# AdaLN, gated recurrence, MLP and conditioned feed-forward on one core: the MLP output made with features on the partitions, and x1 kept in that form for the first feed-forward layer

## The chip, the cores and the metric

The kernel runs on one core of one Trainium2 chip. The metric is the device time of one execution in microseconds (us). The reported time is the median of three runs.

## The reference, cut to what matters

Two sequences of 2048 tokens with 512 features each pass through three stages. Stage 1 is a modulated linear layer and a gated linear recurrence; its result with the residual added is `hs2`. Stage 2 and 3, where the change lies, are

```python
# stage 2, the MLP: x1 is the result
h   = rms_norm(hs2) * norm2_w
g   = gelu(h @ mlp_gate_w.T + mlp_gate_b)
f   = h @ mlp_fc_w.T + mlp_fc_b                 # both 3*512 wide
x1  = x + hs2 + (g * f) @ out_w.T + out_b       # x is the kernel's input
# stage 3, the conditioned feed-forward; _ln(x, g, b) is a layer norm with gain and bias
h = _ln(_ln(x1, pw_g[pathway], pw_b[pathway]), cp_g[compartment], cp_b[compartment])
t = _ln(x1, tm_g[time], tm_b[time]);  s = _ln(x1, ms_g[scale], ms_b[scale])
m, n, r = (x1 + condition_vector[i] for i in range(3))
w = softmax(aw)
cat = concat(w0*h, w1*t, w2*m, w3*n, w4*r, w5*s)
u   = _ln(silu(cat @ int_W1 + int_b1) @ int_W2 + int_b2, int_g, int_be)
out = x1 + int8_matmul(u, rhs)
```

m, n and r are x1 with a vector added, so their three weights are mixed into one and the first layer has four operands: x1, h, t and s.

Products are made in three passes of split operands (high times high, high times low, low times high), so each product of a 128x128 block with 512 columns is three matmuls.

## The kernel before, in words

Everything is cut in eight blocks of 512 tokens (`NB = 8`, `BT = 512`). A block is four tiles of 128 tokens (`TT`) or four tiles of 128 features (`KT`). All five engines run programs written out by hand, joined by semaphores that count up. The functions `two_ahead` and `blocks` (lines 88 and 106) run the first and the last blocks as straight code and those between in a loop, and pass `prev` (a block before this one exists) and `nxt` (one follows) to each body. Stage 2 is `mlp_half` (line 714 on), stage 3 is `conditioned_ffn` (line 1124 on). Stage 3 begins inside the last MLP block: its `early(j)` parts prepare weights and tables, one part behind each feature tile j.

**An MLP block.** TensorE goes through j = 0 to 11 (`FT`), the feature tiles of the 1536 wide layer. For each j it makes the gate product (12 matmuls, `product`, line 848), the fc product (12 matmuls), and then the output product of the tile before (`project_out(j - 1)`, line 863, 12 matmuls). The output product takes `pr` (the split activations) as the stationary operand and `out_w` as the moving one, so its four banks `A[t]` hold tokens on the partitions. `hs2` lies with features on the partitions; `to_tokens` (lines 867 to 878) turns it by 16 transposes per block, four after j = 4, four after j = 5 (`T_AT`), eight after the loop. VectorE adds them to the tile `xt` (128 tokens by 512 features, four of them), into which SyncE has loaded the block of x (line 813), and at the end of the block adds `A[t]` (line 1098). SyncE stores `xt` to `x1_d` in memory (line 820). ScalarE makes Gelu (line 971) and the high part of the product (line 975); VectorE the product (line 1072) and the low part (line 1075).

**SyncE's order in an MLP block** (`body`, lines 810 to 820): wait for the store of the block before, load x, load the next `hs2`; in the last block then `early()` of stage 3 (line 1347), which loads small tables, x1 of block 0, and, once gate and fc of j = 3 are done, the six weights of the condition networks (lines 1362 and 1365: three loads, together 1024 KB, then three of 1024 KB each); then the store of x1. TensorE's part `early(4)` waits for the first three of these six.

**A feed-forward block.** The first layer is a sum over 16 steps `s`: four of x, four of h, and four each of t and s in turn. Each step needs its operand with features on the partitions, split in a high part (ScalarE, `front_high`, line 1650) and a low part (VectorE, `front_low`, line 2036). TensorE makes each by four transposes (`emit`, line 1432): the kinds are "tx" (of x1), "th", "tt", "ts". The 16 of "tx" for the next block stand between the last of the first layer (`main_last`, line 1485, 48 matmuls) and the second layer (`second`, line 1503, 48 matmuls). The second layer ends in the banks `A[t]`, VectorE takes them out (`take_u`, line 2053, semaphore `u_evac`), and the first step of the next block (`main`, line 1466) waits for `u_evac` of each bank before it overwrites it. VectorE's order at the end of a block (lines 2122 to 2127):

```python
            hidden(b)
            if nxt:
                for s in range(XF):          # XF = 4
                    front_low(b + 1, s)
                h_product(b + 1)
                take_u(b)
```

x1 is loaded again in rows (`x1t`, line 1307) for the layer norm, and in `x_residual` tiles (line 1321) for the last addition. GpSimd gathers the time and scale rows by indirect transfers (line 1871) while this goes on.

## Time and profile before

| what | us |
|---|---|
| median of 3 runs | 1853.86 |
| lowest, highest run | 1853.76, 1854.52 |
| the profiled execution, whole | 1854.19 |
| its span, first to last instruction | 1851.1 |
| TensorE busy in the span | 1817.9 |
| VectorE busy | 997.0 |
| ScalarE busy | 733.5 |
| GpSimd busy | 502.6 |

The whole time is 3.1 us more than the span. A time inside the span is counted from its first instruction. Busy time of TensorE is an upper figure, since its matmuls overlap; the distance between the starts of two groups says what a group costs in a stream. The attention stage runs to about 480 us, the eight MLP blocks to about 1285 us, the feed-forward blocks to the end.

### The profile page before, as it was taken

What the parts mean: (1) busy time and instruction counts of PE and PEld (TensorE: products, weight loads), DVE (VectorE), ACT (ScalarE), POOL (GpSimd) and SP (SyncE); (2) the same over time, 40 slices, a digit from 0 to 9 for tenths busy, and PEclk for the clock granted to TensorE, in tenths of its full rate; (3) what the DMA queues carried; (4) which work ended last, traced back from release to release, by engine and by line L of the source; (5) the groups of instructions that cost most, each with busy time, mean ns of one, the idle gap of its engine ahead of it and who ended that gap; (6) DMA issues with size and microseconds to landing.
All of it is one profiled execution on the core that took longest, in us unless ns stands there. A gap on an engine that the chain in (4) does not pass through costs nothing. (4 is left out here: it accounts for less than half of the span.)

```text
span 1851.1 us, 23492 instructions
## 1 busy us (share of the span) xinstructions
PE 1817.9 (98%) x8410; PEld 1483.9 (80%) x8410; DVE 997.0 (54%) x1644; ACT 733.5 (40%) x1117; POOL 502.6 (27%) x502
## 2 busy tenths in 40 slices
PE   7999999999999999999999999999899999999996
PEld 6888888888888888888888888876788888888884
DVE  6767676757743434224242434337775666666555
ACT  6655555556532222222222212224353543533433
POOL 0121222112100000000000000006677876877742
PEclk9999999999999999999999999999999999999998
DMA  5011111013401010101001010453335334324401
GB/s 196 1 46 46 45 45 34 13 46 125 171 1 69 1 69 1 70 1 42 27 3 67 1 69 0 131 192 119 128 126 162 103 125 147 125 92 160 136 12 46
DMA packets 62199, 138.40 MB, mean 75 GB/s; under 512 B 5490, under 2 KB 5746, under 8 KB 62116
## 3 DMA queue, kind: packets, MB, share of 16 engines
q1 hardware_dynamic: 49812, 94.24, 14.8%
q0 software_dynamic: 11776, 41.95, 7.1%
q8 instruction: 58, 0.95, 0.2%
q10 hardware_dynamic: 528, 1.05, 0.2%
q14 instruction: 25, 0.20, 0.0%
HBM read 112.06 MB, written 25.17 MB: 74 GB/s over the span
## 5 line engine op out<-in xcount | busy, mean ns | idle before, releaser
L291 PE MATMUL bank<-h_parts,gate_w 128*128 128x512 f32 x1536 | 351.5, 390 | 0.2 <-DVE h_parts L588 0.2
L291 PEld LDWEIGHTS bank<-h_parts,gate_w 128*128 128x128 f32 x1536 | 288.1, 188 | 61.9 <-issue 1.0
L1072 DVE SCALAR_TENSOR_TENSOR product_full<-bank,vec_sb,gelu 128x512 f32<-128x512 f32 x96 | 72.0, 750 | 408.6 <-PE bank L848 361.4
L1466 PE MATMUL bank<-operand_parts,int_w 128*128 128x512 f32 x1152 | 283.6, 396 | 3.1 <-DVE operand_parts L2036 3.0
L863 PE MATMUL bank<-mlp_out_w,product_parts 128*128 128x512 f32 x1152 | 280.6, 392 | 0.0
L848 PE MATMUL bank<-h_parts,mlp_gate_w 128*128 128x512 f32 x1152 | 276.9, 389 | 0.9 <-DVE h_parts L1055 0.9
L848 PE MATMUL bank<-h_parts,mlp_fc_w 128*128 128x512 f32 x1152 | 276.8, 389 | 0.0
L848 PEld LDWEIGHTS bank<-h_parts,mlp_gate_w 128*128 128x128 f32 x1152 | 216.1, 188 | 46.5 <-issue 1.7
L863 PEld LDWEIGHTS bank<-mlp_out_w,product_parts 128*128 128x128 f32 x1152 | 214.0, 188 | 49.1 <-issue 4.2
L1466 PEld LDWEIGHTS bank<-operand_parts,int_w 128*128 128x128 f32 x1152 | 214.1, 189 | 47.7 <-issue 3.2
L848 PEld LDWEIGHTS bank<-h_parts,mlp_fc_w 128*128 128x128 f32 x1152 | 216.2, 188 | 44.9
L1853 POOL TENSOR_TENSOR fence<-minus_half 128x1 f32<-128x1 f32 x32 | 9.7, 304 | 711.0 <-DVE id_row L2145 707.7
L971 ACT ACTIVATE gelu<-bank,vec_sb 128x512 f32<-128x512 f32 x96 | 66.2, 689 | 281.1 <-PE bank L848 278.5
L975 ACT ACTIVATE product_parts<-product_full 128x512 fp32r<-128x512 f32 x96 | 60.7, 632 | 287.1 <-DVE product_full L1072 284.4
L2036 DVE TENSOR_TENSOR operand_parts<-bank,operand_parts 128x512 fp32r<-128x512 f32 x128 | 85.4, 682 | 73.2 <-ACT operand_parts L1650 73.2
L528 POOL TENSOR_TENSOR decay_sq<-decay 128x512 f32<-128x512 f32 x32 | 37.8, 1180 | 301.6 <-DVE decay L601 301.6
L1075 DVE TENSOR_TENSOR product_parts<-product_full,product_parts 128x512 fp32r<-128x512 f32 x96 | 66.5, 693 | 68.6 <-ACT product_parts L975 68.6
L1485 PE MATMUL bank<-operand_parts,int_w 128*128 128x512 f32 x384 | 90.5, 394 | 0.1
L1503 PE MATMUL bank<-int_w,hidden_parts 128*128 128x512 f32 x384 | 89.0, 391 | 0.0
L1485 PEld LDWEIGHTS bank<-operand_parts,int_w 128*128 128x128 f32 x384 | 72.0, 188 | 16.2 <-issue 0.5
L1650 ACT ACTIVATE operand_parts<-bank 128x512 fp32r<-128x512 f32 x128 | 71.6, 590 | 32.3 <-PE bank L1432 32.2
L1503 PEld LDWEIGHTS bank<-int_w,hidden_parts 128*128 128x128 f32 x384 | 71.6, 188 | 14.5
(272 smaller groups left out, 2307.0 us busy)
## 6 DMA issues: line engine op xcount, KB each, us to landing
xin<-xT SPq DMA_DIRECT2D x8, 1024.0 KB, 7.0
hs_d<-u SPq DMA_DIRECT2D x8, 1024.0 KB, 5.0
x_tiles<-x SPq DMA_DIRECT2D x8, 1024.0 KB, 5.9
x_d<-x_tiles SPq DMA_DIRECT2D x8, 1024.0 KB, 4.5
x_tiles<-x_d SPq DMA_DIRECT2D x8, 1024.0 KB, 8.0
out<-u_tiles SPq DMA_DIRECT2D x32, 256.0 KB, 5.0
raw_w<-int_W SPq DMA_DIRECT2D x7, 1024.0 KB, 7.9
x_residual<-x_d SPq DMA_DIRECT2D x28, 256.0 KB
```

Source lines behind the costliest of these rows:

```text
L291: i = pe.matmul(bank[:], gw[:, w, s, k, m * P:(m + 1) * P], hr[:, q, t, k, :], start=k == 0 and n == 0, stop=k == KT - 1 and n == 2)
L848: i = pe.matmul(bank[:], (gw, fw)[w][j // KT][:, s, k, (j % KT) * P:(j % KT + 1) * P], hr[:, t, k, :], start=k == 0 and n == 0, stop=k == ...
L863: i = pe.matmul(A[t][:], pr[:, j % 2, s, t * P:(t + 1) * P], ow[j // KT][:, w, j % KT, :], start=j == 0 and n == 0, stop=j == FT - 1 and n ...
L971: act.activation(gg[:], G[j % 2][:], ACT.Gelu, bias=v("mlp_gate_b", j)).then_inc(g_evac, 1)
L975: act.activation(pr[:, j % 2, 0, :], pf[:], ACT.Copy).then_inc(p_high, 1)
L1072: dve.scalar_tensor_tensor(out=pf[:], in0=FB[j % 2][:], scalar=v("mlp_fc_b", j), in1=gg[:], op0=ALU.add, op1=ALU.mult).then_inc(p_full, 1)
L1075: dve.tensor_tensor(pr[:, j % 2, 1, :], pf[:], pr[:, j % 2, 0, :].bitcast(F32), ALU.subtract).then_inc(p_low, 1)
L1466: i = pe.matmul(A[m][:], w1[OPER[o]][:, a, k, m * P:(m + 1) * P], op[:, s % 4, c, :], start=s == 0 and n == 0, stop=False)
L1485: i = pe.matmul(A[m][:], w1[OPER[o]][:, a, k, m * P:(m + 1) * P], op[:, s % 4, c, :], start=False, stop=s == NS - 1 and n == 2)
L1503: i = pe.matmul(A[t][:], zr[:, a, k, t * P:(t + 1) * P], w2[:, c, k, :], start=k == 0 and n == 0, stop=k == KT - 1 and n == 2)
L1650: act.activation(op[:, s % 4, 0, :], bank(kind, k)[:], ACT.Copy).then_inc(S["op_high"], 1)
L2036: dve.tensor_tensor(op[:, s % 4, 1, :], bank(FRONT[o], k)[:], op[:, s % 4, 0, :].bitcast(F32), ALU.subtract).then_inc(S["op_low"], 1)
```

## The change

The output product of the MLP has its operands exchanged: `out_w` is the stationary operand and `pr` the moving one, so the banks `A[c]` hold features on the partitions. The last tile's product signals after each bank. x is loaded transposed (`xT`), `hs2` is added to it without a transpose, with the bias in the same instruction (two at j = 6, two at j = 8). x1 is stored with features on the partitions (`x1T_d`), and in the next MLP block its rows are made by 16 transposes, after j = 1, 2, 3, 4, copied out by ScalarE and stored to `x1_d`. For the last MLP block this is done in the first feed-forward block. SyncE's order in the block becomes: load `hs2`, (last block: small loads of stage 3), wait for the store and for the block's transposes, load x, wait for the copies, store the rows, (last block: the weights of stage 3), wait and store x1. The squares, the mean and the normalisation for the next block come at j = 6 and 9 instead of 5 and 7.

In the feed-forward part the "tx" transposes are gone. The four x operands are read from memory: columns 0 and 1 of the next block early in a block, columns 2 and 3 at its end, by transfers of 256 KB that ScalarE issues into the two halves of `xs` once the low parts of columns 0 and 1 are made. VectorE makes the first two low parts, two tiles of the h product, the second two low parts, two tiles of the h product. Some semaphores are merged, with no change of order.

```diff
@@ MLP, numbers @@
-    SQ = 5
-    MS = 8
-    T_AT = {4: 0, 5: 1}
+    SQ = 6
+    MS = 10
+    T_AT = {1: 0, 2: 1, 3: 2, 4: 3}
+    R2_AT = {6: (0, 1), 8: (2, 3)}
+    OB = FT + KT - 1
@@ MLP, sync_program, body @@
+            if prev and nxt:
+                sp.wait_ge(r2, KT * b)
+                load(b + 1, 1 - q)
+            if not nxt:
+                last_small()
             if prev:
                 sp.wait_ge(x_stored, 16 * b)
-            sp.dma_start(xt[:], x_nat[:, bass.ds(TT * b, TT), :]).then_inc(x_loaded, 16)
-            if prev and nxt:
                 sp.wait_ge(t_ps, TT * b)
-                load(b + 1, 1 - q)
+            sp.dma_start(xt[:], xT[:, :, bass.ts(b, BT)]).then_inc(x_loaded, 16)
+            if prev:
+                sp.wait_ge(t_evac, TT * b)
+                sp.dma_start(x1_d[:, bass.ds(TT * (b - 1), TT), :], rows_of[:]).then_inc(t_stored, 16)
             if not nxt:
                 last_early()
-            sp.wait_ge(r1, TT * (b + 1))
-            sp.dma_start(x1_d[:, bass.ds(TT * b, TT), :], xt[:]).then_inc(x_stored, 16)
+            sp.wait_ge(r1, KT * (b + 1))
+            sp.dma_start(x1T_d[:, :, bass.ts(b, BT)], xt[:]).then_inc(x_stored, 16)
@@ MLP, tensor_program @@
-            for t in range(TT):
+            for c in range(KT):
                 for n, (s, w) in enumerate(PASSES):
-                    i = pe.matmul(A[t][:], pr[:, j % 2, s, t * P:(t + 1) * P], ow[j // KT][:, w, j % KT, :],
+                    i = pe.matmul(A[c][:], ow[j // KT][:, s, j % KT, c * P:(c + 1) * P], pr[:, j % 2, w, :],
                                   start=j == 0 and n == 0, stop=j == FT - 1 and n == 2)
-            i.then_inc(o_ps, 1)
...
+                if j == FT - 1 or c == KT - 1:
+                    i.then_inc(o_ps, 1)
+
+        def to_tokens(b, j):
+            t = T_AT[j]
+            pe.wait_ge(r1, KT * b)
+            pe.wait_ge(g_evac, FT * b + j + 1)
             for k in range(KT):
-                i = pe.transpose(T[t][:, k * P:(k + 1) * P], z[q][:, k, t * P:(t + 1) * P], ident[:])
+                i = pe.transpose(G[j % 2][:, k * P:(k + 1) * P], xt[:, k, t * P:(t + 1) * P], ident[:])
             i.then_inc(t_ps, 1)
...
-                if j in T_AT:
-                    to_tokens(b, q, T_AT[j])
+                if prev and j in T_AT:
+                    to_tokens(b, j)
...
-            for t in range(2, TT):
-                if not nxt:
-                    ready(FT)
-                to_tokens(b, q, t)
-            if not nxt:
-                tokens()
@@ MLP, scalar_program @@
+                act.wait_ge(t_stored, 16 * (b - 1))
...
+        def evacuate_rows(b, j):
+            t = T_AT[j]
+            act.wait_ge(t_ps, TT * (b - 1) + t + 1)
+            act.wait_ge(h_low, KT * (b + 1))
+            act.activation(rows_of[:, t, :], G[j % 2][:], ACT.Copy).then_inc(t_evac, 1)
@@ MLP, vector_program @@
-            for k in range(KT):
-                dve.tensor_scalar(z[q][:, k, :], z[q][:, k, :], v("out_b", k), None, ALU.add).then_inc(zb_done, 1)
...
+        def add_hs2(b, q, ks):
+            dve.wait_ge(x_loaded, 16 * (b + 1))
+            for k in ks:
+                dve.scalar_tensor_tensor(out=xt[:, k, :], in0=z[q][:, k, :], scalar=v("out_b", k), in1=xt[:, k, :],
+                                         op0=ALU.add, op1=ALU.add).then_inc(r2, 1)
@@ feed-forward, sync_program @@
-                    sp.wait_ge(S["tx_ps"], KT * (b + 1))
...
-        def early():
+        def early_small():
...
-            sp.wait_ge(mlp["tokens"], TT * (NB - 1))
+            sp.wait_ge(mlp["hs2"], KT * (NB - 1))
+            sp.wait_ge(mlp["tok_stored"], 16 * (NB - 2))
             load(0)
+
+        def early():
             sp.wait_ge(mlp["gate"], LASTJ + KT)
             sp.wait_ge(mlp["fc"], LASTJ + KT)
...
+            for k in range(2, KT):
+                sp.dma_start(xs_first[:, k - 2], x1T_d[:, k, bass.ts(0, BT)]).then_inc(first_loaded, 16)
+            sp.wait_ge(tb_ps, 1)
+            for k in range(2):
+                sp.dma_start(xs[:, k], x1T_d[:, k, bass.ts(0, BT)]).then_inc(xs_loaded[k], 16)
+            sp.wait_ge(S["xh_done"], TT)
+            load(1)
@@ feed-forward, tensor_program @@
+        def last_tokens(ts):
+            pe.wait_ge(mlp["x1"], KT * NB)
+            for t in ts:
+                for k in range(KT):
+                    i = pe.transpose(ring[2 + t % 2][:, k * P:(k + 1) * P], xt[:, k, t * P:(t + 1) * P], ident[:])
+                i.then_inc(mlp["tokens"], 1)
...
-            if nxt:
-                for n in range(NI, len(items)):
-                    item(b, q, n, prev)
@@ feed-forward, scalar_program @@
+        def load_x(b, k):
+            if k < 2:
+                act.wait_ge(S["op_low"], NS * (b - 1) + k + 3)
+            else:
+                act.wait_ge(S["op_low"], NS * b + k - 1)
+            act.dma_start(xs[:, k % 2], x1T_d[:, k, bass.ts(b, BT)]).then_inc(xs_loaded[k % 2], 16)
...
             if nxt:
-                for s in range(XF):
-                    front_high(b + 1, s)
+                x_high(b + 1, 0)
+                x_high(b + 1, 1)
+                load_x(b + 1, 2)
+                load_x(b + 1, 3)
             if not prev:
                 h_centre(b + 1)
-                rhs_round(range(KT))
+                rhs_round(range(2))
+            if nxt:
+                x_high(b + 1, 2)
+                x_high(b + 1, 3)
@@ feed-forward, vector_program @@
-                for s in range(XF):
+                for s in range(0, XF, 2):
                     front_low(b + 1, s)
-                h_product(b + 1)
+                    front_low(b + 1, s + 1)
+                    h_product(b + 1, [s, s + 1])
                 take_u(b)
```

## Rows read from the trace of the kernel before

**Rows 1.** The page, busy time, share of the span and count by engine.

```profile
PE 1817.9 (98%) x8410; PEld 1483.9 (80%) x8410; DVE 997.0 (54%) x1644; ACT 733.5 (40%) x1117; POOL 502.6 (27%) x502
```

**Rows 2.** TensorE's waits: us in total, times, longest us.

```profile
PE bank L1437 <- ACT q_tile L1680: 11.4, 4, 5.5
...
PE bank L1432 <- DVE operand_parts L2036: 2.8, 1, 2.8
```

**Rows 3.** Chain that ended last, around the "tx" transposes: start, us, what.

```profile
1469.72 10.93 PE bank L1485 x48
...
1482.40 10.89 PE bank L1503 x48
```

**Rows 4.** Timeline of TensorE, last MLP block, j = 4: start, us, what.

```profile
1204.06 0.60 PE L877 MATMUL bank<-ident_sb,hs_odd 128*128 128x128 f32 x4
1204.59 1.90 PE L1561 MATMUL bank<-cond_w,states_sb 128*32 128x512 f32 x8
```

**Rows 5.** Timeline of ScalarE, the same place: the high part of j = 4.

```profile
1205.10 0.63 ACT L975 ACTIVATE product_parts<-product_full 128x512 fp32r<-128x512 f32 x1 [2.88 <-DVE product_full L1072]
```

**Rows 6.** Timeline of SyncE's issues, the weights of the condition networks.

```profile
1196.13 1.36 SPq L1362 DMA_DIRECT2D cond_w<-W  x3
1197.54 1.59 SPq L1365 DMA_DIRECT2D cond_w<-W  x3
```

**Rows 7.** Line 1365 alone: issue to landing of its three loads.

```profile
DMA to landing us min/median/max: 8.0/10.2/12.3
```

**Rows 8.** Timeline of TensorE, first feed-forward block, around one idle stretch.

```profile
1304.58 4.58 PE L1466 MATMUL bank<-operand_parts,int_w 128*128 128x512 f32 x12 [2.31 <-DVE operand_parts L2036]
1309.00 1.03 PE L1432 MATMUL bank<-ident_sb,time_scale_rows 128*128 128x128 f32 x8
```

**Rows 9.** Stretch table there: us, PE PEld DVE ACT POOL busy, clock, DMA share, GB/s.

```profile
1306.00:1309.00 3.00, 3.00 (x11) 2.29 (x10) 3.00 (x6) 0.00 (x0) 1.98 (x3) 0.63 0.85 267
```

**Rows 10.** Chain there: the last gather before the first feed-forward block's t products.

```profile
1288.55 9.45 DMA time_scale_rows<-ts_rows,row_now
```

**Rows 11.** Timeline of ScalarE and VectorE, end of a feed-forward block.

```profile
1481.41 0.63 ACT L1717 ACTIVATE hidden_parts<-hidden_full 128x512 fp32r<-128x512 f32 x1
...
1482.07 0.69 DVE L2042 TENSOR_TENSOR hidden_parts<-hidden_full,hidden_parts 128x512 fp32r<-128x512 f32 x1 [1.91 <-ACT hidden_parts L1717]
1482.68 2.48 DVE L2036 TENSOR_TENSOR operand_parts<-bank,operand_parts 128x512 fp32r<-128x512 f32 x4
1485.08 2.49 DVE L2026 TENSOR_TENSOR h_norm<-h_norm,cp_rows 128x512 f32<-128x512 f32 x4
1491.29 2.73 DVE L2053 TENSOR_TENSOR u_tiles<-bank,int_rows 128x512 f32<-128x512 f32 x4 [3.73 <-PE bank L1503]
```

**Rows 12.** Timeline of SyncE and GpSimd, the same stretch: transfers and who used them.

```profile
1474.30 0.33 SPq L1321 DMA_DIRECT2D x_residual<-x_d  x1
...
1475.55 0.33 SPq L1321 DMA_DIRECT2D x_residual<-x_d  x1
...
1484.95 0.41 SPq L1307 DMA_DIRECT2D x_tiles<-x_d  x1
...
1477.70 1.30 POOL L1919 TENSOR_TENSOR u_tiles<-u_tiles,x_residual 128x512 f32<-128x512 f32 x1
...
1482.44 1.47 POOL L1919 TENSOR_TENSOR u_tiles<-u_tiles,x_residual 128x512 f32<-128x512 f32 x1 [1.42 <-DMA x_residual<-x_d]
...
1484.23 0.98 POOL L1871 DMA_INDIRECT time_scale_rows<-ts_rows,row_now  x1 [0.16 <-issue]
1490.35 5.05 POOL L1878 TENSOR_TENSOR time_scale_rows<-time_scale_rows,xhat 128x512 f32<-128x512 f32 x4 [5.13 <-DMA time_scale_rows<-ts_rows,row_now]
```

**Rows 13.** The page, issues of SyncE: count, KB each, median us to landing.

```profile
x_tiles<-x SPq DMA_DIRECT2D x8, 1024.0 KB, 5.9
...
x_d<-x_tiles SPq DMA_DIRECT2D x8, 1024.0 KB, 4.5
x_tiles<-x_d SPq DMA_DIRECT2D x8, 1024.0 KB, 8.0
```

247 lines of the change are left out of this document (130 added, 117 removed).

## The prediction

> **What bounds the kernel now.** I read the page's busy times first: TensorE is busy for 1817.9 of 1851.1 us, no other engine for more than 54% [rows 1]. So nearly every microsecond of TensorE's stream counts, and the rest is about 33 us of waits. The table of its waits says where they are: 11.4 us at the very end for the quantised tiles [rows 2], and at the start of the feed-forward part single waits of 2.8 us before L1432 [rows 2] and 2.31 us before L1466 [rows 8]. In the middle of the program TensorE doesn't stand still. Two things therefore decide: what the change takes out of TensorE's stream, and whether TensorE meets a wait that it doesn't have now. For the second I read the timelines of the queues and of the engines that feed TensorE, in the places where the change touches them: j = 4 of the last MLP block, the start of the feed-forward part, and the end of a feed-forward block.
>
> **What the change takes away.** The matmuls of the output product stay the same in number and shape, only with their operands exchanged: nothing. Of the transposes, "tx" goes. Its price is read from the chain: the 48 matmuls before it end at 1469.72 + 10.93 = 1480.65, the 48 after it begin at 1482.40, so 16 transposes cost 1.75 us [rows 3]. The transposes of `hs2` in MLP block b become transposes of x1 in block b + 1, the same 16. The first MLP block has none any more: minus 1.75 us, with nothing in its place. The last MLP block's come in the first feed-forward block, where the "tx" of block 0 went. That leaves seven places, between the two layers of feed-forward blocks 0 to 6, at 1.75 us each, 12.25 us at most. VectorE loses the additions of the bias and ScalarE gains four copies per MLP block of about 0.6 us in some 98 us (432 matmuls at 10.93 / 48 us) [rows 3, 5]; both are idle for a good part of an MLP block, so I cost that at nothing. If this cover were gone, the Gelu of the next tile would be late, and with it the gate bank that TensorE wants two tiles later.
>
> **What it adds, first place: j = 4 of the last MLP block.** TensorE's `early(4)` waits for the first three weights of the condition networks (together 1024 KB). Now SyncE issues them at 1196.13, as soon as j = 3 is through, and TensorE takes them at 1204.59 without a wait [rows 4, 6]. In the changed order SyncE has to pass two more waits before it comes to them: for all the block's transposes, the last of which end after j = 4, and for ScalarE's copy of the last one. TensorE makes those transposes directly ahead of its wait. So the whole of the transfer lies open, and two others of 1024 KB (x in, rows out) are ahead of it in the same queue. In the times of the trace of before: transposes done 1204.6, x issued 1204.7; the high part ends at 1205.10 + 0.63 = 1205.73 [rows 5], the copy behind it at about 1206.35, the rows are issued at 1206.4, the three weights from 1206.9 to 1208.2. How long do 3072 KB in a row take? The best row is the burst of now: the first 1024 KB are issued from 1196.13, then three of 1024 KB from 1197.54; the second of these is issued near 1198.05 and lands 10.2 us later, at 1208.25 [rows 6, 7]. That is the third 1024 KB, 12.1 us after the first issue. From 1204.7 this gives 1216.8, an idle time of 12.2 us. From below: the last weight is issued at about 1207.7, and the shortest landing of 256 KB in the rows is 3.4 us (third place, below): 1211.1, 6.5 us idle. From above: x, rows and weights one after the other at what each size takes alone, 5.9 + 4.5 + 5.9 us [rows 13]: 1221.0, 16.4 us. I take 12.2, since its row has the same sizes and the same queue.
> The Trainium skill ("DMA: Bandwidth & Descriptors", Anatomy of one DMA) gives some 2 us fixed and the bytes at 436 GB/s for a transfer: by it the 3 MB would land 9.2 us after the first issue, 2.9 us earlier than the burst of this trace; by the one the sum below would be 6.7, by the other 9.6.
> Then the clock. After an idle time of 2.31 us TensorE's 12 matmuls at 1304.58 run until 1309.00, 4.42 us, where a group of 12 takes 2.73 in a stream (10.93 by 4) [rows 3, 8]; the granted clock was 0.63 between 1306 and 1309, so most of that time was at the level of 1.2 GHz and not at that of 2.4 [rows 9]. That is 1.7 us more. I add 1.7 (between 0 and 3.4, twice the row). This place costs 13.9 us.
> The rest of `early` hangs on TensorE's own progress and moves with it.
>
> **Second place: the first feed-forward block.** The first steps hang on the gather of the time and scale rows, 9.45 us from 1288.55 [rows 10], which GpSimd issues at a pace of its own; what TensorE does ahead of that is not on the path. So the 16 transposes removed here and the 16 added cost nothing. The load of x1 for block 1 goes out earlier and leaves the transfer engines to the gather: 1024 KB less beside it. The burst moved four such loads in 14.8 us, 3.7 each [rows 6, 7]; some of it is made up for by the 512 KB of columns, so I take a third, minus 1.3, between minus 3.7 and plus 1.8 (half of 3.7, if the columns weigh and the load doesn't).
>
> **Third place: the end of a feed-forward block, six times.** Columns 2 and 3 of x are loaded only when the low parts of columns 0 and 1 are made, and VectorE takes the second layer's result (`take_u`) behind them. The first step of the next block waits for `take_u`. Step by step [rows 11]: the last low part of the hidden layer ends at 1482.76; with 0.62 us each (2.48 by 4) the low parts of columns 0 and 1 end at 1483.4 and 1484.0; ScalarE issues the second load at 1484.05. With a landing time L: the high part 0.63, the low part 0.62, two tiles of the h product 1.24, the first tile of `take_u` 0.68. So the first bank is free at 1487.2 + L. TensorE's second layer now ends at 1480.65 + 10.89 = 1491.54. A wait begins when L is over 4.3 us. What is L? Idle engines: an x_residual tile, also 256 KB, issued at 1474.30 was there at 1477.70 for GpSimd's addition without a wait, 3.4 us or less. Busy ones: the tile issued at 1475.55 was there at 1482.44, 6.9 us. The gather of 1484.23 runs in just this stretch, beside the load of 1024 KB of 1484.95, and lands by 1490.35, 6.1 us [rows 12]. I take 6.1: two columns are together as large as this gather and issued within 0.2 us of it. The wait is 1.8 us, and the saving of 1.75 is gone: plus 0.05 each, 0.3 for six, with ends of minus 1.75 (L of 3.4) and plus 0.85 (L of 6.9). At the end of block 0 ScalarE has other work between the column pairs (centring h, rounding of the weights) that has to be done anyway, which covers the load: minus 1.5 there, once.
> The Trainium skill's figures for a transfer (the same page and section) would make L 2.6 us, no wait, and a sum lower by 10.8; no load in these rows came so soon.
>
> **The sum.** Minus 1.75 (first MLP block), plus 13.9 (weights), minus 1.3, minus 1.5, plus 0.3: plus 9.6. The profiled execution took 1854.2, its span 1851.1 and 3.1 around it; the median of the runs is 0.3 lower. The forecast is 1863.5 us. A measurement of this kernel tells a change from none at about 0.2%, 3.7 us.
>
> **The rivals.**
> *Columns in time.* L is 3.4 to 4.3 us, TensorE doesn't wait at the ends of blocks, and the six ends give 10.5 us: plus 9.6, minus 0.3, minus 10.5 is minus 1.2, a time of 1853.0, no change. For it: the loads are issued 0.9 us before the one of 1024 KB. Against: the stretch already has a transfer that takes 6.1 us. Chance 0.18.
> *Short wait for the weights.* This is the one that ends faster: the three weights, small ones, land at the lower bound, 6.5 us idle and no slow clock after it, with the columns in time as above. Its place is j = 4 of the last MLP block, its price 6.5 for 13.9 us: minus 1.2, minus 7.4 is minus 8.6, 1845.6. It decides from the point where idle time and clock together are under 11.4 us: then the sum passes minus 3.7. Against it: the order in one queue has held in the burst, 8.0, 10.2, 12.3 us [rows 7]. Chance 0.08.
> *Columns later than that.* The load of 1024 KB and the gather both get ahead; L is 8.0 us, the median landing of that load [rows 13], and the wait 3.7 us. Six times 1.9 more is 11.4: 1875, and 1885 if each brings the 1.7 us of slow clock that followed 2.31 us of idling [rows 8]. Against: a column is a quarter of the load's size. Chance 0.16.
> *The exchange does not do what it says*, that is, features on the partitions cost more matmul time: the first layer has its weights stationary and the second its operand, both 48 matmuls in 10.9 us [rows 3], so I give it nothing.
>
> **How the numbers follow.** Forecast 0.58, the others as given. By the bounds of the weights alone (idle 6.5 to 16.4, clock 0 to 3.4: minus 7.4 to plus 5.9) the forecast's own range is 1856 to 1869.5. The overall range takes in the first rival and comes close to the third: 1851 to 1874; left out are the second and most of the third, and a little of the first. Faster by over 3.7 us: 0.10 (the second rival, and the low edge of the first). Within 3.7: 0.18. Slower: 0.72 (the rest of the forecast's cases and the third).
>
> **What would show it.** In the changed profile, TensorE's waits should have a new line at the 128x32 matmuls of the condition networks (now L1561), for a transfer, of about 12 us, once; a stretch of lower granted clock behind it; and six waits of 1 to 3 us before the first step of a feed-forward block, released by VectorE's `take_u`. The "tx" rows should be gone, the second layer should follow the first at once. The first would be wrong if SyncE's three issues came before the copies; the third if `take_u` started within 10.5 us of the second layer's start. The prediction as a whole is wrong if the weights land in under 8 us after TensorE asks, or if L is not near 6.

## The result, and the profile after

The changed kernel takes 1917.43 us, median of four runs (1915.46 to 1921.83), against 1853.81 us of the kernel before in the same session: a ratio of 1.035, 95% interval 1.0327 to 1.0372. It is slower by 63.6 us, where 9.6 was forecast; the time lies above the range of 1851 to 1874. The profiled execution took 1921.8 us and its span is 1920.0, 68.9 more than the span before.

Where do the 68.9 us lie? TensorE's timeline of the kernel before, at four points that both programs have: the first matmul of the last MLP block, the first of the feed-forward part, the second layer of block 0 and that of the last block (start, us, engine, line, operation, tensors, count):

```profile
1168.69 1.52 PE L848 MATMUL bank<-h_parts,mlp_gate_w 128*128 128x512 f32 x6
...
1285.52 5.69 PE L1466 MATMUL bank<-operand_parts,int_w 128*128 128x512 f32 x24
...
1347.23 11.14 PE L1503 MATMUL bank<-int_w,hidden_parts 128*128 128x512 f32 x48
...
1815.42 11.04 PE L1503 MATMUL bank<-int_w,hidden_parts 128*128 128x512 f32 x48
```

The same four points of the kernel after:

```profile
1170.52 1.75 PE L857 MATMUL bank<-h_parts,mlp_gate_w 128*128 128x512 f32 x7
...
1301.27 6.12 PE L1504 MATMUL bank<-operand_parts,int_w 128*128 128x512 f32 x24 [1.28 <-DVE x_columns L1098]
...
1364.36 11.04 PE L1541 MATMUL bank<-int_w,hidden_parts 128*128 128x512 f32 x48
...
1884.35 11.04 PE L1541 MATMUL bank<-int_w,hidden_parts 128*128 128x512 f32 x48
```

Up to the last MLP block +1.83. Through that block to the feed-forward part 130.75 for 116.83, +13.92. Through the first block to its second layer 63.09 for 61.71, +1.38. From there to the second layer of the last block 519.99 for 468.19, +51.80. Behind it nothing (35.65 for 35.68). So three quarters of the loss lie in the stretch with the seven block ends, which the forecast had at 0.3 us for six and minus 1.5 for that of block 0. From second layer to second layer it is +1.6 us over the end of block 0 (69.55 for 67.94) and +50.2 over the other six, 8.4 each.

The table of TensorE's waits after (engine and tensor that waited, line, released by, us in total, times, longest); of before only the line for the quantised tiles is the same [rows 2]:

```profile
PE bank L1504 <- DVE u_tiles L2111: 48.2, 7, 8.0
PE bank L1596 <- DMA cond_w<-W: 11.9, 1, 11.9
PE bank L1475 <- ACT q_tile L1724: 11.4, 4, 5.5
PE bank L857 <- issue: 3.4, 2, 2.6
```

The two waits that the prediction named are there, at the top: for `take_u` (now L2111) seven times, 48.2 us, and for the weights once, 11.9 us. Of the seven, the one at the end of block 0 is 2.46 us, the other six are 6.95 to 8.04 us, where six of 1 to 3 us were forecast.

**The weights.** TensorE's timeline around j = 4 of the last MLP block, then SyncE's queue beside it, then the granted clock in windows of 5 us (stretch, length, busy time of PE, PEld, DVE, ACT and POOL, each with its instructions, PEclk, DMA share, GB/s):

```profile
1207.31 0.60 PE L882 MATMUL bank<-ident_sb,x_columns 128*128 128x128 f32 x4
1219.81 3.59 PE L1596 MATMUL bank<-cond_w,states_sb 128*32 128x512 f32 x8 [11.91 <-DMA cond_w<-W]
1223.33 3.70 PE L872 MATMUL bank<-product_parts,mlp_out_w 128*128 128x512 f32 x12
```

```profile
1207.98 0.37 SPq L822 DMA_DIRECT2D x_columns<-xT  x1
1209.48 0.39 SPq L825 DMA_DIRECT2D x_d<-x_rows  x1
1209.97 3.01 SPq L1372 DMA_DIRECT2D cond_w<-W  x3
```

```profile
1215.00:1220.00 5.00, 0.19 (x3) 0.22 (x6) 0.00 (x0) 0.00 (x0) 1.86 (x4) 0.50 1.03 382
1220.00:1225.00 5.00, 5.00 (x12) 1.75 (x9) 0.00 (x0) 0.00 (x0) 1.97 (x3) 0.52 1.05 397
```

The transposes end at 1207.9, x goes out at 1207.98, the rows behind ScalarE's copy at 1209.48, the three weights from 1209.97; the wait is 11.91 us, forecast 12.2. From the issue of x to the first weight matmul it is 11.8 us (the burst of before: 12.1 [rows 6, 7]). By the Trainium skill's figure in the prediction ("DMA: Bandwidth & Descriptors", Anatomy of one DMA) the estimate was 9.2. The trace doesn't agree; but that section gives its figure for a transfer that GpSimd issues, and these are SyncE's, with three more of 1024 KB issued behind them from 1213.02. While TensorE stood the granted clock fell to 0.50, which is 1.2 GHz, and it was at 0.52 until 1225; the eight weight matmuls took 3.59 us for 1.90 [rows 4], and the twelve behind them 3.70, where the same twelve took 2.99 in the trace of before (at 1206.42): 2.4 us together. So this place cost 14.3 us, forecast 13.9. That the whole block shows +13.92 is in part luck: the 16 "tx" transposes of block 0, which stood at its end before, have left it (about 1.8 us less), and a wait of 1.28 us for the last tile of x1 has come in.

**A block end.** The timeline of all engines at the end of block 1, without weight loads and without lines that the reading doesn't need (in brackets the idle time before, and what ended it):

```profile
1433.91 11.04 PE L1541 MATMUL bank<-int_w,hidden_parts 128*128 128x512 f32 x48
1435.50 0.69 DVE L2100 TENSOR_TENSOR hidden_parts<-hidden_full,hidden_parts 128x512 fp32r<-128x512 f32 x1 [1.89 <-ACT hidden_parts L1762]
1435.57 1.77 POOL L1976 TENSOR_TENSOR u_tiles<-u_tiles,x_residual 128x512 f32<-128x512 f32 x1 [1.10 <-DMA x_residual<-x_d]
1436.11 2.38 DVE L2094 TENSOR_TENSOR operand_parts<-x_columns,operand_parts 128x512 fp32r<-128x512 f32 x2
1438.01 0.43 SPq L1315 DMA_DIRECT2D x_tiles<-x_d  x1
1438.05 1.06 ACTq L1672 DMA_DIRECT2D x_columns<-x1T_d  x2
1438.41 1.28 DVE L2084 TENSOR_TENSOR h_norm<-h_norm,cp_rows 128x512 f32<-128x512 f32 x2
1443.71 0.63 ACT L1682 ACTIVATE operand_parts<-x_columns 128x512 fp32r<-128x512 f32 x1 [7.20 <-DMA x_columns<-x1T_d]
1446.74 0.63 ACT L1682 ACTIVATE operand_parts<-x_columns 128x512 fp32r<-128x512 f32 x1 [2.40 <-DMA x_columns<-x1T_d]
1446.95 6.27 POOL L1935 TENSOR_TENSOR time_scale_rows<-time_scale_rows,xhat 128x512 f32<-128x512 f32 x4 [7.61 <-DMA time_scale_rows<-ts_rows,row_now]
1447.40 1.37 DVE L2094 TENSOR_TENSOR operand_parts<-x_columns,operand_parts 128x512 fp32r<-128x512 f32 x1 [2.33 <-ACT operand_parts L1682]
1448.69 3.41 DVE L2084 TENSOR_TENSOR h_norm<-h_norm,cp_rows 128x512 f32<-128x512 f32 x2
1452.03 2.47 DVE L2111 TENSOR_TENSOR u_tiles<-bank,int_rows 128x512 f32<-128x512 f32 x4
1452.85 7.62 PE L1504 MATMUL bank<-operand_parts,int_w 128*128 128x512 f32 x24 [7.90 <-DVE u_tiles L2111]
```

Read it from the top. The second layer starts at 1433.91 and would hand over at 1444.95. VectorE's last low part of the hidden layer ends at 1436.19. The low parts of columns 0 and 1 then take 2.38 us for two, beside a GpSimd addition; the four of before took 2.48 us beside the same addition [rows 11, 12]. ScalarE issues column 2 at 1438.05 and column 3 at 1438.67; SyncE has just issued the 1024 KB of x1 rows, at 1438.01. Column 2 is there at 1443.71, column 3 at 1446.74. The low part takes 1.37, and the second pair of h products 3.41 us (the first pair, 1438.41, took 1.28), beside GpSimd's four products of 6.27 us. Only then `take_u` starts, at 1452.03, 7.1 us after the banks were full; TensorE has waited 7.90. The clock follows (same columns as above):

```profile
1450.00:1455.00 5.00, 2.15 (x5) 1.79 (x6) 5.00 (x8) 0.00 (x0) 3.42 (x3) 0.51 0.14 51
```

It is at 0.51 when TensorE starts again, and its 24 matmuls take 7.62 us. In the trace of before the same 24 of the same block took 5.61:

```profile
1426.14 5.61 PE L1466 MATMUL bank<-operand_parts,int_w 128*128 128x512 f32 x24
```

That is 2.0 us more; at the six ends it is 1.9 to 2.3 us, 12.4 in all.

### The profile page after: what moved, and what is told of

It is laid out like the page before. It is cut to its first block and busy times, and to the rows that moved or that the text cites. A ratio compares the mean times of both kernels' runs of the same rounds, so it can differ in the third digit from the quotient of the medians.

```text
span 1920.0 us, 23465 instructions
## 1 busy us (share of the span) xinstructions
PE 1822.4 (95%) x8274; PEld 1480.7 (77%) x8282; DVE 997.2 (52%) x1612; ACT 752.2 (39%) x1149; POOL 512.8 (27%) x502
## 5 line engine op out<-in xcount | busy, mean ns | idle before, releaser
L1504 PE MATMUL bank<-operand_parts,int_w 128*128 128x512 f32 x1152 | 296.8, 409 | 52.6 <-DVE u_tiles L2111 48.2
L1504 PEld LDWEIGHTS bank<-operand_parts,int_w 128*128 128x128 f32 x1152 | 222.8, 197 | 103.1 <-issue 37.5
L872 PE MATMUL bank<-product_parts,mlp_out_w 128*128 128x512 f32 x1152 | 280.6, 394 | 0.0
L872 PEld LDWEIGHTS bank<-product_parts,mlp_out_w 128*128 128x128 f32 x1152 | 213.8, 188 | 50.2 <-issue 5.9
L2094 DVE TENSOR_TENSOR operand_parts<-bank,operand_parts 128x512 fp32r<-128x512 f32 x96 | 65.7, 684 | 93.8 <-ACT operand_parts L1689 93.7
L1523 PE MATMUL bank<-operand_parts,int_w 128*128 128x512 f32 x384 | 90.4, 394 | 0.1
L1523 PEld LDWEIGHTS bank<-operand_parts,int_w 128*128 128x128 f32 x384 | 72.0, 188 | 16.2 <-issue 0.5
L1689 ACT ACTIVATE operand_parts<-bank 128x512 fp32r<-128x512 f32 x96 | 55.6, 592 | 50.7 <-PE bank L1470 50.6
```

The source lines that it names most:

```text
L872: i = pe.matmul(A[c][:], ow[j // KT][:, s, j % KT, c * P:(c + 1) * P], pr[:, j % 2, w, :], start=j == 0 and n == 0, stop=j == FT - 1 and n ...
L1504: i = pe.matmul(A[m][:], w1[OPER[o]][:, a, k, m * P:(m + 1) * P], op[:, s % 4, c, :], start=s == 0 and n == 0, stop=False)
L1523: i = pe.matmul(A[m][:], w1[OPER[o]][:, a, k, m * P:(m + 1) * P], op[:, s % 4, c, :], start=False, stop=s == NS - 1 and n == 2)
L1689: act.activation(op[:, s % 4, 0, :], bank(kind, k)[:], ACT.Copy).then_inc(S["op_high"], 1)
L2094: dve.tensor_tensor(op[:, s % 4, 1, :], x_columns(b, k) if o == "x" else bank(FRONT[o], k)[:], op[:, s % 4, 0, :].bitcast(F32), ALU.subtra ...
```

## The experiments

Fifteen kernels were run. Where lines of an edit are left out, `...` stands. The two places were first mended alone and together.

**Weights early** (`w_early`): SyncE issues the six weights before the block's x and rows. The edit moves the line where the function `early` begins, so that the six loads belong to `early_small`, which SyncE runs first.

```diff
             load(0)
-
-        def early():
             sp.wait_ge(mlp["gate"], LASTJ + KT)
             sp.wait_ge(mlp["fc"], LASTJ + KT)
...
             for i in range(3):
                 sp.dma_start(mw2[i][:], ins[f"W2_{i}"].rearrange("(k p) o -> p k o", p=P)).then_inc(ld["mw2"], 16)
+
+        def early():
             sp.wait_ge(mlp["out"], LASTO + KT)
```

> One edit to the changed kernel: in the last MLP block SyncE issues the six weights of the condition networks once j = 3 is through, as in the kernel before, ahead of its waits for the transposes and the copies. Theory A (the place of the issues in SyncE's order is the whole cost): the 11.9 us wait goes, and 2.4 us of slow matmuls after it: 14.3 us less, about 1903 us. Rival: x and the rows, now behind 4 MB of weights, come late in turn, the squares or the addition of hs2 wait, and 5 us or more of it stay: over 1908 us.

Measured 1905.84 us, 11.6 less, and no wait for `cond_w` is left. In its trace the last MLP block, from 1167.04 to the first feed-forward matmul at 1283.53, takes 116.49 us for 130.75, 14.3 less: this place is about what it was summed at, 13.9. The medians differ by 2.7 less than the block does; the runs of the kernel after lie 6.4 us apart, and the profiled one is the slowest.

**The u tiles ahead of the late columns** (`u_first`), and both edits together (`both`):

```diff
-                for s in range(0, XF, 2):
-                    front_low(b + 1, s)
-                    front_low(b + 1, s + 1)
-                    h_product(b + 1, [s, s + 1])
+                front_low(b + 1, 0)
+                front_low(b + 1, 1)
+                h_product(b + 1, [0, 1])
                 take_u(b)
+                front_low(b + 1, 2)
+                front_low(b + 1, 3)
+                h_product(b + 1, [2, 3])
```

> One edit to the changed kernel: VectorE takes the second layer's result (take_u) ahead of the second pair of low parts and h products, instead of behind them. Theory A (the wait is one of order: take_u stands behind two transfers in VectorE's queue): the 48.2 us that TensorE waits for take_u and the slow clock behind each wait (about 2 us, 7 times) go, some 62 us: about 1856 us. Theory B (columns 2 and 3 themselves are late): the wait only moves, to the first step that needs column 2, and most of it stays: over 1890 us. Theory C (VectorE is slowed by work on the shared memory in this stretch): half at most comes back, about 1885 us.

> The two edits together. Theory A: the two costs are independent, 1917 less 62 less 14 is about 1841 us, 0.7% faster than the kernel before, which is the 12.25 us of the removed transposes in the feed-forward part and 1.9 us of the first MLP block. Rival: something else of the change costs too (the transfers, ScalarE's copies, the loop), and it ends level with the kernel before, 1850 us or more.

1887.88 and 1873.39 us: `u_first` gave 29.6 us where theory A wanted some 62. Each edit helps, but both together leave 19 us over the kernel before. Taking `take_u` out of the queue behind the transfers moved a part of the wait: the late low parts and products now hold up what stands behind them on VectorE. The line of the wait table of `both` that took the place of the 48.2 us:

```profile
PE bank L1504 <- DVE operand_parts L2094: 15.6, 7, 3.9
```

**All h products behind the first two low parts** (`h_first`), with low parts 2 and 3 still ahead of `take_u`:

```diff
-                for s in range(0, XF, 2):
-                    front_low(b + 1, s)
-                    front_low(b + 1, s + 1)
-                    h_product(b + 1, [s, s + 1])
+                front_low(b + 1, 0)
+                front_low(b + 1, 1)
+                h_product(b + 1)
+                front_low(b + 1, 2)
+                front_low(b + 1, 3)
                 take_u(b)
```

> One edit to the changed kernel: all four tiles of the h product ahead of the second pair of low parts; take_u stays last. If the path behind the columns has the h product at its undisturbed 1.24 us for two tiles, 7 times 1.2 us come back, 9 us: about 1909 us. If it is the 3.4 us that the profile shows in six of the seven blocks, because GpSimd multiplies the time and scale rows at the same time, then about 21 us come back, a little more with the clock: 1896 us or less.

1894.50 us: 22.9 less than after, by moving two instructions of 128x512 in each block. The late pair's 3.4 us beside GpSimd was on the chain.

**No late columns** (`no_col`): the order is left as it is, and the kernel leaves out the loads of columns 2 and 3 in blocks 1 to 7, so that their parts are made from the old content of the buffers. And **the load of x1 rows late** (`x1_late`):

```diff
-                act.wait_ge(xs_loaded[k % 2], 16 * (2 * b + k // 2))
+                act.wait_ge(xs_loaded[k % 2], 16 * (b + 1))
...
                 x_high(b + 1, 1)
-                load_x(b + 1, 2)
-                load_x(b + 1, 3)
```

```diff
                     sp.wait_ge(S["xh_done"], TT * (b + 1))
+                    sp.wait_ge(xs_loaded[1], 16 * (2 * b + 1))
                     load(b + 1)
```

> The kernel after, order and place of the weights as they are, but columns 2 and 3 of the blocks 1 to 7 are not loaded: the high and low parts of x columns 2 and 3 are made from the buffers of columns 0 and 1 as they stand, so this kernel leaves out half of the columns of x in those blocks. It takes away the two transfers on the chain at a block end and leaves VectorE's order alone. Theory A (the chain is first bank free = landing of column 3 plus the late pair of products): six ends give back their 6.9 us of wait and 2.2 us of slow clock, 1917 - 55 = 1862 us. Rival (VectorE's and GpSimd's own work at the end sets the chain, and the landing is only the releaser that came last by little): above 1895 us.

> The kernel after, but the 1,024 KB load of the next block's rows of x1 is issued only when column 3 of the block has landed; in the kernel after it is issued within a microsecond of the loads of columns 2 and 3, whose landings take 5.7 and 7.7 us. Theory A (the columns are late because they share the DMA engines with this load, which a landing of 2.6 us for 256 KB in a free moment supports): the landings fall to 3 to 4 us, each of six ends gets 3 to 4 us shorter, 1893 us. Rival (the landing is long by its own cost or by the other transfers): the landings stay at 6 to 8 us and the time stays within 5 us of 1917.

`no_col`: 1868.47 us, 49 less. The timeline of VectorE at one of its block ends, with GpSimd's addition:

```profile
1430.00 2.39 DVE L2092 TENSOR_TENSOR operand_parts<-x_columns,operand_parts 128x512 fp32r<-128x512 f32 x2
1430.20 1.64 POOL L1974 TENSOR_TENSOR u_tiles<-u_tiles,x_residual 128x512 f32<-128x512 f32 x1 [1.11 <-DMA x_residual<-x_d]
1432.32 1.28 DVE L2082 TENSOR_TENSOR h_norm<-h_norm,cp_rows 128x512 f32<-128x512 f32 x2
1433.52 1.28 DVE L2092 TENSOR_TENSOR operand_parts<-x_columns,operand_parts 128x512 fp32r<-128x512 f32 x2
1434.72 1.28 DVE L2082 TENSOR_TENSOR h_norm<-h_norm,cp_rows 128x512 f32<-128x512 f32 x2
1436.85 2.73 DVE L2109 TENSOR_TENSOR u_tiles<-bank,int_rows 128x512 f32<-128x512 f32 x4 [0.84 <-PE bank L1541]
```

The second pair of products takes 1.28 here: with no transfer ahead of it, it has run before GpSimd's products begin, at 1439.70. So the columns cost twice, by their landing and by pushing the pair into GpSimd's time. The low parts show the same: two from SBUF take 2.39 us beside GpSimd's addition (1430.00) and 1.28 without one (1433.52). `x1_late`: 1896.23 us, 21.2 less. The median landing of a column went only from 6.6 to 5.4 us, less than theory A wanted, though the time came near its 1893; GpSimd's wait for its gathered rows fell too, from 57.9 to 40.8 us in all. The load of 1024 KB beside them delayed both.

**The three together** (`hx_w`: the edits of `w_early`, `h_first` and `x1_late`), with low parts 2 and 3 ahead of `take_u` as in the forecast:

> The kernel after with the three edits that were each tried alone, two of them aimed at the block end: weights early (11.6 us alone), all h products behind low parts 0 and 1 (22.9 us alone), the 1,024 KB load of rows of x1 behind the landing of column 3 (21.2 us alone). Low parts 2 and 3 still stand ahead of the u tiles, so this is the order in which the prediction summed the block end, with a landing and a product pair near the sizes that it took. If the terms add (the late pair and the landing stand one behind the other on one chain): 1917.4 - 11.6 - 22.9 - 21.2 = 1862 us. If the prediction's own sum holds with its 0.3 us an end: 1849 us. If the two edits of the block end take away the same microseconds: 1880 us.

1854.05 us (ratio to before 0.9998, 0.9986 to 1.0010). The parts alone add up to 55.7 us, together they give 63.4. The forecast's own sum without its 13.9 us for the weights is 1849.6, 4.4 less than measured, and the expectation from adding up was 1862. At the block end read, column 3 lands 5.3 us after its issue (forecast 6.1) and the four h products take 2.49 us. Its wait table has this left at the block ends:

```profile
PE bank L1505 <- DVE u_tiles L2112: 8.0, 5, 2.7
```

Five waits of 1.6 us on average; the prediction had six of 1.8.

**All of it off the path.** `hu_w`: weights early, and the order low 0, low 1, four h products, `take_u`, low 2, low 3. `slot3_w`: the same, with a third column buffer of 2 KB for column 2, so that only column 3 waits for one. The edit of `slot3_w` against `hu_w`:

```diff
+    xs_third = at("x1_columns_third", [P, BT], HR_AT + 4 * KB)
...
+                    load_x(b + 1, 2)
...
                 x_high(b + 1, 1)
-                load_x(b + 1, 2)
+                x_high(b + 1, 2)
                 load_x(b + 1, 3)
...
                 front_low(b + 1, 1)
+                front_low(b + 1, 2)
                 h_product(b + 1)
                 take_u(b)
-                front_low(b + 1, 2)
                 front_low(b + 1, 3)
```

> The kernel after with two edits: the three conditioning weights are issued before the last block's early rows (as in the run that moved only them), and VectorE's order at a block end is low parts 0 and 1, all four h products, the four tiles of the second layer's result, low parts 2 and 3. The run that had both places mended but two h products left behind the late low parts took 1873.4 us, with 15.6 us of waits of the feed-forward matmuls for low parts and 8.1 us for the h products (the late pair took 3.48 us beside GpSimd's time-scale products). Theory A (what is left is VectorE's chain at the block end, of which the late pair is the head): the 8.1 us go and about half of the 15.6, since the moments of the u tiles start some 3.5 us sooner: 1858 us, still not faster than the 1854 before. Rival (the order does not matter, what is left is the late landing of columns 2 and 3 itself): 1870 to 1875 us. Third (everything at a block end is covered, as the prediction's rival had it): 1841 us.

> As the run with h products and the u tiles ahead, but a third buffer of 2 KB holds column 2 as well, so that three of the four columns are loaded while the block before is at work and only column 3 waits for a buffer (that of column 0). Order on VectorE: low parts 0, 1 and 2, all h products, the four u tiles, low part 3. Theory A (the buffers for columns, two for four, are the cost, together with the order): no wait for a column is left at the block ends, 1848 us, at the level of the kernel before or a little under it. Rival (the landings were already covered once the order was changed): the same as the run beside it, within 3 us.

1865.19 and 1859.62 us: neither reached what was expected. What holds them? A timeline of `slot3_w`, from a block end on:

```profile
1429.25 5.26 POOL L1935 TENSOR_TENSOR time_scale_rows<-time_scale_rows,xhat 128x512 f32<-128x512 f32 x4 [7.34 <-DMA time_scale_rows<-ts_rows,row_now]
1433.59 1.03 PE L1473 MATMUL bank<-ident_sb,h_norm 128*128 128x128 f32 x8
1438.73 0.20 POOL L1941 TENSOR_TENSOR mean_shift<-mean_shift,rstds 128x4 f32<-128x4 f32 x1
1438.97 1.52 ACT L1698 ACTIVATE u_tiles<-u_tiles,mean_shift,rstds 128x512 f32<-128x512 f32 x2 [10.45 <-POOL mean_shift L1941]
1440.39 0.58 ACT L1689 ACTIVATE operand_parts<-bank 128x512 fp32r<-128x512 f32 x1
1441.00 0.69 DVE L2094 TENSOR_TENSOR operand_parts<-bank,operand_parts 128x512 fp32r<-128x512 f32 x1 [3.99 <-ACT operand_parts L1689]
1441.84 1.40 PE L1507 MATMUL bank<-operand_parts,int_w 128*128 128x512 f32 x5 [0.88 <-DVE operand_parts L2094]
```

The second layer started at 1417.26, the h products are done before 1425, and TensorE waits for no column. But the first h column, whose transposes are done at 1434.6, is copied by ScalarE only at 1440.39, behind the centring of the u tiles, which waits until 1438.73 for GpSimd's mean shift. GpSimd's time-scale products began at 1429.25, behind a gather, 12.0 us after the second layer's start; in the kernel before it is 8.2 to 9.4 us at the two ends read. My reading was that the "tx" transposes gave this chain 1.75 us more in every block of the kernel before, and that with them gone it sets the pace. So the copy was put ahead of the centring in ScalarE's body (`slot3_ws`, `hu_ws`, and as a control `before_s`), and the late load of x1 rows was added (`slot3_wsx`, `hu_wsx`).

```diff
-                if prev and U_AT <= s < U_AT + 2:
-                    u_centre(b - 1, [2 * (s - U_AT), 2 * (s - U_AT) + 1])
...
                 if XF <= s + AHEAD < NS:
                     front_high(b, s + AHEAD)
+                if prev and U_AT <= s < U_AT + 2:
+                    u_centre(b - 1, [2 * (s - U_AT), 2 * (s - U_AT) + 1])
```

> The kernel with three column buffers and early weights, 1859.6 us, and one edit more: at each step of the first layer ScalarE copies the high part of the next operand column ahead of the centring of the u tiles of the block before, where it stood behind it. In that kernel's trace the first h column waited on ScalarE behind a centring that waits for GpSimd's mean shift (an idle of 10 to 16 us there), and the first-layer matmuls waited 0.9 to 2.4 us once a block for its low part, 13.2 us in all. Theory A (what is left is that chain, which the 1.9 us of transposes at the block end had covered in the kernel before): the 13 us go and the time is 1847 us, 0.4% under the kernel before. Rival (GpSimd's chain itself is late, and the wait moves on to the products made from the u tiles or to the second h column): 1855 to 1860 us.

> The same edit of ScalarE's order in the kernel with two column buffers, all h products and the u tiles ahead of low parts 2 and 3, and early weights: 1865.2 us without it, with 21.7 us of waits of the first-layer matmuls for low parts. Theory A (with the order mended two buffers are enough, as the landings of 3.4 us stand behind 11 us of second-layer matmuls and 11 us of first-layer ones): 1849 us, within 3 us of the run with three buffers. Rival (the late columns 2 and 3 cost what separates 1865 from 1860): 1852 to 1855 us.

> The kernel before with the edit of ScalarE's order alone, as a control. Its trace shows no wait of the first-layer matmuls for operand parts: 1854 us within 2 us, by theory A. If it gets faster by more than 3 us, the order of ScalarE is worth something by itself, and the part of the change in the mended version's time is smaller by as much.

> The version with three column buffers, early weights and ScalarE's order, with the 1,024 KB load of the next rows of x1 issued only behind the landing of column 3. In the kernel after this shortened the landings and gave 21 us. Theory A (here every landing is covered): no difference, within 2 us of the run without it. Rival (the gathers of the time-scale rows, which GpSimd awaits for 7 us at the block end beside the same transfers, land sooner too, and GpSimd's chain with them): 2 to 6 us less. Third (the load itself comes late for the moments of x): slower by 2 us or more.

The kernel before took 1853.45 us in the same session.

| kernel | us | ratio to before, 95% |
|---|---|---|
| `slot3_ws` | 1855.93 | 1.0015 (1.0006 to 1.0024) |
| `hu_ws` | 1860.32 | 1.0032 (1.0020 to 1.0044) |
| `before_s` | 1852.21 | 0.9996 (0.9987 to 1.0005) |
| `slot3_wsx` | 1846.45 | 0.9966 (0.9954 to 0.9978) |

The order of ScalarE gave 3.7 and 4.9 us of the 13 and 16 expected. For `slot3_ws` the rival held, that GpSimd's chain itself is late; `hu_ws` came out above its rival's 1852 to 1855 as well. The late load gave the rest, 9.5 us, more than its rival's 2 to 6: GpSimd's wait for the time-scale rows fell from 53.3 to 40.7 us. The last two runs asked whether two buffers do, and whether the kernel before can have the same gain; there the load of x rows is held back until the first tile of the second layer is done.

```diff
                     sp.wait_ge(S["xh_done"], TT * (b + 1))
+                    sp.wait_ge(S["u_ps"], TT * (b - 1) + 1)
                     load(b + 1)
```

> The version with two column buffers, all h products and the u tiles ahead of low parts 2 and 3, early weights and ScalarE's order (1860.3 us), with the late load of the rows of x1. Theory A (the third buffer is worth little once GpSimd's gathers and the columns land sooner): 1848 to 1850 us, the two buffers enough to be faster than before. Rival (two late columns on the queue cost GpSimd's gathers as much as they did): 1854 us or more.

> The kernel before with ScalarE's order and its own 1,024 KB load of the next rows of x held back until the first tile of the second layer is done (some 7 us later than it was), as a control for the version that is 7 us faster than the kernel before. Theory A (in the kernel before GpSimd's chain is covered, so that nothing is gained by sooner gathers): 1852 us, within 2 us. Rival (the gathers set something there too): 2 us or more under 1852, and the gain of the mended version is in part no gain of the change. Third (the rows come late for the moments of x): above 1855 us.

`hu_wsx`: 1845.16 us, ratio 0.9950 (0.9935 to 0.9964), the fastest of all and 15.2 less than `hu_ws`, where theory A wanted 10 to 12. `before_sx`: 1852.16, ratio 0.9990 (0.9982 to 0.9999), no gain over `before_s`, although GpSimd's wait for its gathered rows fell there too (51.3 to 36.4 us). So the 7.0 us between the two are put down to the change. VectorE's order wasn't tried in the kernel before, where TensorE has no wait at these block ends. One block end of `hu_wsx`, where both late columns stand behind `take_u`:

```profile
1426.78 2.73 DVE L2112 TENSOR_TENSOR u_tiles<-bank,int_rows 128x512 f32<-128x512 f32 x4 [2.05 <-PE bank L1542]
1427.53 0.63 ACT L1683 ACTIVATE operand_parts<-x_columns 128x512 fp32r<-128x512 f32 x1 [1.73 <-DMA x_columns<-x1T_d]
1428.62 5.61 PE L1505 MATMUL bank<-operand_parts,int_w 128*128 128x512 f32 x24
1429.42 3.10 DVE L2095 TENSOR_TENSOR operand_parts<-x_columns,operand_parts 128x512 fp32r<-128x512 f32 x2
```

The second layer started at 1417.74 and ends at 1428.78; `take_u` began at 1426.78, column 3 landed at 1427.53, and TensorE goes on at 1428.62 without a wait. The distance of second layers:

```profile
1417.74 11.04 PE L1542 MATMUL bank<-int_w,hidden_parts 128*128 128x512 f32 x48
1483.68 11.04 PE L1542 MATMUL bank<-int_w,hidden_parts 128*128 128x512 f32 x48
1548.90 11.04 PE L1542 MATMUL bank<-int_w,hidden_parts 128*128 128x512 f32 x48
```

65.94 and 65.22 us, where the kernel before has 66.98 from 1415.17 to 1482.15. The 1.75 us of "tx" are gained in full in the second pair. The low parts behind `take_u` took 1.55 us each (1429.42), beside GpSimd's products, and cost TensorE nothing.

## Why the prediction was wrong

Right were the direction and the two places where TensorE would come to wait. Step by step:

- **First MLP block**, forecast minus 1.75: it took 98.45 us for 100.31, minus 1.86. Not foreseen were two waits of TensorE for "issue", at two of the turns of the loop over MLP blocks, 3.4 us together; behind the longer one, 2.63 us, its 12 matmuls took 4.58 for 2.88. The profile doesn't say what TensorE waited for, no run aimed at it, and they vary (1.9 to 3.6 us in the variants); this is left open.
- **The weights**, forecast 13.9: held, 11.91 of wait and 2.4 by the clock.
- **First feed-forward block**, forecast minus 1.3 (a third of 3.7 is 1.2), measured plus 1.4. Its longest wait is now one of 3.0 us for operand parts, where before it was 2.31 [rows 8]; where that comes from wasn't tried.
- **End of block 0**, forecast minus 1.5: this failed too, at plus 1.6. ScalarE's other work was to cover the load; but column 3 was there only at 1374.64, 7.4 us after the pair's first issue, TensorE waited 2.46, and its next 24 matmuls took 7.33 us, 1.7 more than 5.61.
- **Block ends**, forecast 0.3 for six: this step failed, measured +50.2. The chain was the right one and the formula held; its sizes did not. "First bank free at 1487.2 + L" gave a wait of 1.8, and 7.90 was measured at the end shown. Column 3 landed 3.1 us later than forecast: the last low part of the hidden layer ended at 1436.19, so column 3 was to be issued 1.29 later and to land 6.1 after that, at 1443.6, and came at 1446.74. Its issue was 1.2 late (1438.67, as the low parts took 2.38 for 1.24), and the landing took 8.0. The low part behind it took 1.37 for 0.62, and the pair of h products 3.41 for 1.24. That is 6.1 us. `x1_late` showed the landing, `h_first` the pair, and `hx_w` with both mended came back to waits of 1.6. The forecast had the columns issued 0.9 us ahead of the 1024 KB of x1 rows; at four of the six ends both came behind it. At the last end, which has no such load, column 3 landed in 6.5 us, at the other five in 7.6 to 8.8, and the wait was still 6.95.
- **The clock at the block ends**, forecast at nothing: 1.9 to 2.3 us each, 12.4 in all. I had a price for it, 1.7, in the rival "columns later" and not in the forecast, since I took a wait of 1.8 for too short. The rival's 1885 was the nearest case, and had the landing alone as its mechanism; at a wait of 3.7 us it still fell short, because the products beside GpSimd weren't in it.

Two of the rivals' times, 1853.0 and 1845.6, are added to the profiled execution and not to the median as the forecast is; they should be 0.3 us lower.

Why was the price of the low parts and products wrong? For the low parts I took 0.62 us from rows in which VectorE reads a bank of PSUM and one tile of SBUF. In the changed kernel the low part of x reads two tiles of SBUF. For the products, which read two tiles of SBUF in both kernels, I took 0.62 from a row that ends before GpSimd's products begin [rows 11, 12]. By my own sum the late pair would have run from 1491.4, and GpSimd's products run from 1490.35 to 1495.40 [rows 12]: the collision could be read there. The rows say what it does:

- from a bank: 0.62 each beside GpSimd's addition (low parts [rows 11, 12]) and beside its products (`take_u`, 1452.03, the first two of four);
- from two tiles of SBUF with no arithmetic of GpSimd: 0.64 each (products 1438.41, low parts of `no_col` 1433.52);
- from two tiles of SBUF beside GpSimd: 1.19 each with its addition (1436.11), 1.37 and 1.71 each with its products (low part 1447.40, h products 1448.69).

The Trainium skill ("SBUF — State Buffer", Who interferes with whom) has this as a rule: a VectorE instruction with two inputs in SBUF contends with a GpSimd instruction that reads SBUF, one with a single SBUF input does not. All these rows agree with it. It gives no size, but it would have put the price of the low parts and of the late pair in question.

## What to carry over

Removing work from the bounding engine gains only if the chains that ran beside it were shorter by that much; look for the next one before counting the gain, here GpSimd's gather and mean shift. A transfer that starts late in a block must not stand in an in-order queue ahead of something TensorE waits for, and what queues behind it is pushed into another engine's time. When an operand moves from PSUM to SBUF, VectorE's price for it is another one while GpSimd works, here 1.19 or 1.37 us for 0.62.

## What was not expected of the hardware

- VectorE's products of 128x512 f32 with both inputs in SBUF: 0.64 us each without arithmetic of GpSimd, 1.71 us each beside its products; GpSimd's four took 6.27 us there (1446.95) and 5.05 in the kernel before [rows 12].
- A wait of 7.90 us cost TensorE a further 2.0 us through the clock (granted 0.51), one of 11.91 a further 2.4 us (0.50).
- The issue of one load of 1024 KB, moved a few microseconds in each block with nothing else changed (in the blocks read, from 4.1 to 10.0 us behind the start of the second layer in `x1_late`, from 5.7 to 7.5 in `slot3_wsx`), gave 21.2 us in the one and 9.5 in the other, through the landings of other transfers. In the kernel before a like delay (9.3 us behind the start in `before_sx`) gave nothing.
